# Scores of layers 2 and 3 as sums of one-pass float32r products, with q, k and the row maxima split into halves

## Time and profile before

| | us |
|---|---|
| median of 3 runs | 3493.28 (3492.97 to 3499.72) |
| profiled execution, first to last instruction | 3493.6 |
| of it, from the first to the last maximum of the slots | 1661.1 to 3235.6 |

### The profile page before, as it was taken

One profiled execution on the slowest core, in us unless ns is written; L12 is line 12 of the kernel. 1 busy time (PEld: TensorE's weight loads), 2 busy tenths in 40 slices (PEclk: granted clock), 3 DMA queues, 4 the chain that ended last, 5 costly groups with the idle time before them and its releaser, 6 DMA issues.

```text
span 3493.6 us, 49096 instructions
## 1 busy us (share of the span) xinstructions
PE 3288.6 (94%) x19540; PEld 1805.6 (52%) x19540; DVE 1845.4 (53%) x3843; ACT 1443.6 (41%) x2613; POOL 243.4 (7%) x214
## 2 busy tenths in 40 slices
PE   6899999999889999998999999999999999999887
PEld 3555666656565666666333344444444444453364
DVE  4776544562412232324766765567755666656343
ACT  0344444453412222221355455554555544555433
POOL 1100000100100000001000010010100101001010
PEclk9899999999889999999999999999999999999899
DMA  5200000002000000001000000000000000000000
GB/s 166 90 1 6 8 20 1 23 6 95 16 22 1 0 1 0 1 1 56 1 1 1 1 7 1 4 25 7 7 1 4 22 10 7 1 10 19 7 1 13
DMA packets 57256, 57.99 MB, mean 17 GB/s; under 512 B 17728, under 2 KB 51248, under 8 KB 56764
## 3 DMA queue, kind: packets, MB, share of 16 engines
q1 hardware_dynamic: 57028, 54.79, 5.0%
HBM read 46.89 MB, written 7.89 MB: 16 GB/s over the span
## 4 chain that ended last, share of the span: by engine, by line
PE 88%; DVE 9%; ACT 2%; issue 1%; POOL 0%; DMA 0%; DVEq 0%; SPq 0%; ACTq 0%
PE ps L902 81%; PE ps L1076 3%; DVE max_halves L1565 1%; DVE row_max_cross L1718 1%; PE ps L1203 1%; PE ps L1056 1%; PE ps L1067 1%; DVE big L1590 1%; ACT probs L1944 1%; DVE bn_stats L1619 1%; PE ps L1181 0%; ACT big L1896 0%; DVE bn_stats L1596 0%; DVE xn_tok L1632 0%; DVE big L1724 0%
## 5 line engine op out<-in xcount | busy, mean ns | idle before, releaser
L1896 ACT ACTIVATE big<-ps 128x512 f32<-128x512 f32 x1280 | 687.4, 597 | 826.7 <-PE ps L902 825.9
L902 PE MATMUL ps<-big 32*128 32x512 f32 (+2 forms) x5760 | 940.8, 603 | 16.4 <-DVE row_max L1562 4.3
L1565 DVE TENSOR_REDUCE max_halves<-ps 128x1 f32<-128x512 f32 x1024 | 652.6, 684 | 341.4 <-PE ps L902 340.0
L902 PEld LDWEIGHTS ps<-big 32*128 32x128 f32 (+1 forms) x5760 | 380.8, 188 | 494.5 <-issue 389.6
L902 PE MATMUL ps<-big,probs 128*32 128x512 f32 (+1 forms) x2688 | 379.3, 606 | 8.2 <-ACT big L1896 4.1
L902 PE MATMUL ps<-weights_mlp,big 128*128 128x256 f32 (+1 forms) x1248 | 333.0, 418 | 2.5 <-ACT big L1956 2.5
L902 PEld LDWEIGHTS ps<-weights_mlp,big 128*128 128x128 f32 x1248 | 233.7, 190 | 84.4 <-issue 58.4
L1602 DVE TENSOR_TENSOR x_tok<-ps,x_tok 128x512 f32<-128x512 f32 x112 | 77.2, 690 | 309.0 <-PE ps L902 309.0
L902 PE MATMUL ps<-x_T,weights_mlp 128*128 128x256 f32 x1024 | 231.1, 384 | 2.5 <-ACT x_T L1913 2.3
L1944 ACT ACTIVATE probs<-ps 77x512 f32<-77x512 f32 x384 | 196.1, 591 | 88.3 <-PE ps L902 88.0
L1562 DVE TENSOR_REDUCE row_max<-ps 128x2 f32<-128x512 f32 x256 | 164.6, 684 | 99.7 <-PE ps L902 99.5
(11 more groups left out here) (223 smaller groups left out, 3385.2 us busy)
## 6 DMA issues: line engine op xcount, KB each, us to landing
weights_mlp<-in_L_xcond_mlp_W SPq DMA_DIRECT2D x5, 1024.0 KB, 5.3
weights_mlp<-in_L_xcond_W_mlp SPq DMA_DIRECT2D x5, 1024.0 KB, 5.3
x_tok<-in_x SPq DMA_DIRECT2D x4, 1024.0 KB, 9.4
out_y<-x_tok SPq DMA_DIRECT2D x8, 512.0 KB, 2.9
big<-in_L_xcond_e_w SPq DMA_DIRECT2D x3, 1024.0 KB, 10.1
gates_biases<-mod_rows SPq DMA_DIRECT2D x20, 128.0 KB, 5.0
big<-in_L_xcond_adaLN_W SPq DMA_DIRECT2D x1, 2304.0 KB
kc_groups<-x_tok SPq DMA_DIRECT2D x3, 616.0 KB, 8.4
```

The lines of the kernel that those rows point to most:

```text
L902: return pe.matmul(out, lhsT, rhs, start=first, stop=last)
L1565: dve.tensor_reduce(NMP[:, e, j, qt, hf:hf + 1], PS[:, bank, :], AX.X, ALU.max, negate=True).then_inc(R.frees(key), 1)
L1896: act.activation(PB[:, score % 2, j, :], PS[:, R.bank(key), :], ACT.Exp, scale=SCALE).then_inc(R.frees(key), 1)
```

```diff
-                self.lead = self.per + 2
+                self.split = l == 2
+                self.lead = self.per + (3 if self.split else 2)
...
+            if R.split:
+                return out + [("qk", b, m, a, hf) for m in range(KT) for a, hf in ((1, 0), (1, 1), (0, 0), (0, 1))] + [("v", b, m) for m in range(KT)]
...
+            if kind == "slot" and R.split:
+                return (1.9 if tok[1] is not None else 0.0) + (0.95 if tok[2] is not None else 0.0) + 0.45 * len(tok[4]) + 0.45 * len(tok[5])
             if kind == "slot":
                 return (2.15 if tok[1] is not None else 0.0) + (1.05 if tok[2] is not None else 0.0) + 0.45 * len(tok[4]) + 0.45 * len(tok[5])
...
+                    if tok[0] == "qk" and R.split:
+                        _, b, m, a, hf = tok
+                        n = R.parted.index(tok[1:])
+                        sp.wait_ge(*R.freed(tok))
+                        for x, part in enumerate((0, 1) if a else (0, 1, 0)):
+                            dst = KPd[b, m, :, x, :, hf * HALF:(hf + 1) * HALF] if a else QPd[b, m, hf, :, x]
+                            sp.dma_start(dst, STG[:, n % STAGES, part, :].bitcast(F32)).then_inc(R.part_out[n % STAGES], 16)
+                    if tok[0] == "ld":
+                        n = tok[1]
...
+                        if n >= Q_BLOCKS:
+                            sp.wait_ge(R.pv, (n - Q_BLOCKS + 1) * R.per)
+                        if qh == 0:
+                            for hf in range(NH):
+                                sp.wait_ge(*R.parts_landed(b, m, 1, hf))
...
+                        sp.wait_ge(*R.parts_landed(b, m, 0, qh))
+                        for x in range(2):
+                            sp.dma_start(QR[:, n % Q_BLOCKS, x, :].bitcast(F32), QPd[b, m, qh].rearrange("(j e) x r n -> e j x r n", e=2)[e, :, x:x + 2].rearrange("j x r n -> j (x r) n")).then_inc(R.q_in[n % Q_BLOCKS], 16)
...
+                def by_parts(t, f, half):
...
+                            stationary.append([KR[rows, u, kt * P:(kt + 1) * P]] * 2 + [SUB[rows, :]])
+                            moving.append([QR[rows, n % Q_BLOCKS, 0, :], QR[rows, n % Q_BLOCKS, 1, :], MR[rows, n % 2, :]])
...
+                        stationary.append([QR[rows, n % Q_BLOCKS, x, c:c + P] for x in range(2)])
+                        moving.append([KR[rows, u, hf * HALF:(hf + 1) * HALF]] * 2)
+                    banks = []
+                    for step in range(3):
+                        for i, key in enumerate(keys):
+                            if step == 0:
+                                banks.append(take(key))
+                            if step < len(moving[i]):
+                                last = mm(PS[:, banks[i], :], stationary[i][step], moving[i][step], step == 0, step == len(moving[i]) - 1)
+                                if step == len(moving[i]) - 1:
+                                    done(last, key)
...
+                        elif R.split:
...
+                            dve.wait_ge(R.part_hi, n + 1)
+                            dve.scalar_tensor_tensor(parts[:, 1, :], PS[:, R.bank(tok), 0:w], QB[:, 3 * a, m:m + 1], parts[:, 0, :].bitcast(F32), ALU.add, ALU.subtract).then_inc(R.frees(tok), 1)
...
+                    for n in nms if R.split else ():
+                        if n >= 2:
+                            act.wait_ge(R.pv, (n - 1) * R.per)
+                        act.wait_ge(*R.full(("nm", n)))
+                        copy(MR[:, n % 2, :], PS[:, R.bank(("nm", n)), :]).then_inc(R.frees(("nm", n)), 1)
...
+                            act.wait_ge(*R.full(tok))
+                            if n >= STAGES:
+                                act.wait_ge(*R.parts_landed(*R.parted[n - STAGES]))
+                            act.activation(STG[:, n % STAGES, 0, :], PS[:, R.bank(tok), 0:w], ACT.Identity, bias=QB[:, 3 * a, m:m + 1]).then_inc(R.part_hi, 1)
...
+                    for n in tok[5] if kind == "slot" and R.split else ():
+                        pool.wait_ge(R.nm_f, n + 1)
...
+                        pool.tensor_copy(halves[:, :, ROW_HI:ROW_HI + 4].bitcast(F32R), NMF[:, n % 2]).then_inc(R.nm_h, 1)
+                        pool.wait_ge(R.nm_h, n + 1)
+                        pool.tensor_tensor(halves[:, :, ROW_LO:ROW_LO + 4], NMF[:, n % 2], halves[:, :, ROW_HI:ROW_HI + 4], ALU.subtract).then_inc(R.nm, 1)
```

More of the change, by code:

```diff
@@ L7 @@
 F32 = mybir.dt.float32
+F32R = mybir.dt.float32r
 BF16 = mybir.dt.bfloat16
@@ L459, in slot_token @@
             tails = ((base + t - 2) // R.per,) if 2 <= t < count + 2 and (t - 1) % R.per == 0 else ()
-            nms = ((base + ahead) // R.per - 1,) if 0 < ahead <= count and ahead % R.per == 0 else ()
+            after = ahead - 1 if R.split else ahead
+            nms = ((base + after) // R.per - 1,) if 0 < after <= count and after % R.per == 0 else ()
             return ("slot", base + t if 0 <= t < count else None, base + ahead if ahead < count else None, base + t - 1 if 1 <= t <= count else None, tails, nms)
@@ L551, in open_to @@
                     return rows[tok[-1]] is None
+                if kind == "qk" and R.split:
+                    return True
                 if kind == "qk" and tok[1]:
@@ L577, in slot_ready @@
                 b, g, qh = R.block(fill // R.per)
-                if fill < NB * R.total and fill % R.per == 0 and qh == 0 and g % 2 == 0:
+                if R.split and fill < NB * R.total and fill % R.per == 0:
+                    if ("ld", fill // R.per) not in ended:
+                        return None
+                    times.append(ended["ld", fill // R.per] + 4.0)
+                if not R.split and fill < NB * R.total and fill % R.per == 0 and qh == 0 and g % 2 == 0:
                     for k in R.qk_steps(b, g // 2):
@@ L618, in place, with block_fits @@
                         place(item[0])
+                while R.split and state["ld"] < NB * NG * NH and block_fits(state["ld"]):
+                    state["ld"] += 1
+                    order.append(("ld", state["ld"] - 1))
+                    ended["ld", state["ld"] - 1] = state["now"] + 5.0
+            def block_fits(n):
+                b, g, qh = R.block(n)
+                parts = [("qk", b, g // 2, 0, qh)] + ([("qk", b, g // 2, 1, hf) for hf in range(NH)] if qh == 0 else [])
+                return all(k in ended for k in parts) and (n < Q_BLOCKS or state["t"] > (n - Q_BLOCKS + 1) * R.per)
             def hidden_follows(tok):
@@ L1044, in slot @@
                     for half in range(2):
+                        if R.split:
+                            by_parts(score, fills, half)
+                            if half == 0 and product is not None:
+                                pv(product)
+                            continue
                         if score is not None:
@@ L1066, in slot @@
                             qt = 4 * qh + i
[L1067 removed]
+                            rows = NM[:, q % 2, i:i + P] if R.split else NM[:, 2 * qh + g % 2, qt:qt + P]
+                            last = pe.transpose(PS[:, bank, i * P:(i + 1) * P], rows, ident[:, :])
                         done(last, ("nm", q))
```

81 lines of the change are left out of this document (73 added, 8 removed).

## The result

The changed kernel takes 3471.41 us (median of 6 runs, 3466.34 to 3475.47), the kernel before 3494.59 us beside it (6 runs, 3488.58 to 3500.87): a ratio of 0.9925, 95% interval 0.9906 to 0.9943. It is faster, by 23 us and clear of the interval, where 94 were forecast; the time lies within the stated range (3330 to 3485), the gain is a quarter of the forecast one. The profiled execution has a span of 3464.7 us, 28.9 less than the one before.

The account below looks back on a forecast made before the run. PE was taken to bound the kernel, busy 94% of the span. From 3493.6 us, A -105, B -28, D +29, E +6 and F +5 gave 3400.6, stated as 3400 us, range 3330 to 3485.

Parts of the forecast that it names:

- A: PE's score halves: three rounds of 0.216 us passes, a half 0.86 us in place of 1.07; -105 us.
- Loads inside a half: Weight loads of rounds two and three stay hidden under running passes on PE, costed at nothing.
- the rival built on it: Each round pays 0.10 us for its load, so A and B gain nothing: 3533 us, chance 0.06.
- the slower pass: A float32r pass on PE costs 0.43 us, like a float32 pass: 3695 us, chance 0.07.
- not done: Products run as float32 after all, some 870 us more; left under the slower pass, no chance of its own.
- B: Slots without filler: fourth row gets its bank earlier, slot 3.22 us in place of 3.85; -28 us, bounds 0 and -80.
- F: Maxima split on in-order POOL, so PE's transposes sometimes wait for it: +5 us, 0 to 20.
- E: Later projections: ACT waits for parts to land, holding exponentials and PE: +6 us, 0 to 20.
- 133 waits: PE's waits for exponentials before the change, 110 + 23, 80 us in all; B counted 0.21 us for each.
- that rival: Evacuation by DVE and ACT comes later and eats half of A: 3481 us, chance 0.08.
- D: Start of the region: parts go through DRAM and back before the first maxima and scores: +29 us, 10 to 50.
- 1677 if half of that shows: In D, last landing at 1677 us if half of read-backs' 5.2 us ahead of parts shows, 1683 if all.

Follow-up runs that it names:

- e7: e6 with MLP weights, their biases and the first batch row's cross keys issued behind the second read-back: 3386.67 us, ratio 0.9688.
- e1: Changed kernel with parts laid out in DRAM so part DMAs have 128 or 64 outermost rows, not 8 and 4: 3427.73 us, ratio 0.9815.
- e3: Changed kernel with the two POOL instructions that split the maxima moved to DVE: 3448.51 us, ratio 0.9890.
- e4: Changed kernel with exponentials of layers 2 and 3 on 256 of 512 columns, output not the reference's: 3427.07 us, ratio 0.9808.
- e6: Changed kernel with the edits of e1 and e3, and the first three read-backs later in SP's queue: 3405.51 us, ratio 0.9751.
- e2: Changed kernel without the parts' way through DRAM, fixed rows copied by POOL instead, output not the reference's: 3407.52 us, ratio 0.9762.
- e11: Changed kernel run once more, unedited, one execution: 3474.4 us.
- e10: e6 run once more, unedited, one execution: 3390.2 us.

## Why the prediction was right and wrong

**The direction and the passes (A) were right, the size 13 us off.** A half takes 0.89 us over the trace in place of 0.86: 512 x 0.18 = -92, not -105. The row that failed me is the 0.216 of the earlier trace rows: a float32r pass begins 0.23 to 0.24 after the one before it. I called that row a bf16 product; only its weight loads are bf16, and the columns that it streams stand in the trace before as fp8e4, so it was a farther row than I said:

```profile
80.70 2.17 PE L902 MATMUL ps<-probs,ones_b 128*128 128x512 fp8e4 x8
```

**Loads inside a half were hidden, as I took it.** The first round's loads lie in the open, and the second round begins 0.34 after it; had each round paid like that, the third would begin 0.34 after the second. It begins 0.24 after. The rule that I set against it ("TensorE: Matmul & The Clock Gate" of the Trainium skill, Part 3, The mechanism) doesn't show here, and the rival built on it is out. So are the slower pass and "not done".

**The fourth bank (B) was right in the slot and hardly to be seen in the sum.** The slot without filler took 3.31 where I said 3.22. Summed from each half's first weight load to that of the next thing PE does, halves took 695.7 us before and 604.3 after; less 512 unhindered halves (1.07 and 0.89) that leaves 148 of waiting on either side. In e7, with F gone, E smaller and the clock higher, 116 are left (572.1 - 456): -32. Not all of that is B. Over halves that lie wholly at the higher clock, the waiting is 0.26 us a half before and after, 0.25 in e1, 0.24 in e3 and 0.22 in e7, some 20 us for 512; the rest of the 32 goes with the clock. So some 20 of B's 28 were there, and in the changed kernel the waits that e1 and e3 take away stood in their place. My 133 waits were a little high, too: 7 of the 23 of products are the stops of weight loads, counted twice.

The rows of PE's waits before, over the scored slots (the earlier trace rows shows a shorter stretch):

```profile
PEld ps L902 <- DVE max_halves L1565: 90.0, 121, 4.1
PEld ps L902 <- ACT big L1896: 65.1, 110, 1.6
...
PE ps L902 <- ACT big L1896: 18.7, 27, 1.2
```

With each stop counted once, PE's waits for ACT went from 83 to 91 us, those for DVE's maxima from 92 to 46. So evacuation didn't eat A. The measured time lies in the range that I gave that rival (3455 to 3495, price 3481), but by the start's loss and not by its mechanism. e4 shows what ACT's waits are worth: 44 us, some 9 of them by the clock (24 us less of the low one). That is a bound for a next change.

**The start (D) is the step that failed: +59 for +29, beyond its bound of 50.** The chain as I walked it was right in kind: eight projections, two staging buffers, read-backs ahead of parts in SP's queue. The mis-sized term is the landing. I took 3.0 us from the W_proj load, which is as large but lies across 128 partitions; the parts' DMAs run on 8 and 4 engines and let the waiting engine go 4 to 10 us after their last issue, and four issues took 8.95 us where e1 needs 2.81. So the first maxima, put 21 us later than before, began 49 later (69.1 us into the region in place of 20.0); from there to the first scores the loss was 10, of 8 forecast. With the width mended (e1) landings are near what I had taken, 2.5 to 4.5, the first maxima begin 23 later, and D is 83.3 - 49.4 = +34 against my +29. My upper bound, 50, came from the 616 KB write; it was no bound, since that row told nothing of how a smaller DMA is spread. I had priced a DMA by its size alone. Of the start's 108.8 us, 68 had the lower clock, against 15 of 49.4 before; 44 of them are one stretch from 1674 to 1718 us, in which PE mostly waited. What that cost no run shows.

**The order in SP's queue** I had costed at half, "1677 if half of that shows"; in e1 the fifth part stood ready at 1666.2 and was issued at 1673.6, and e6 got 11 us by moving three read-backs. The weights in front cost 6 more (e7). I had let the first landing take 4.3 from SP's becoming free; I left out that these weights still had to land (ACT had its first landing 2.9 us after the last of four issues in e6, 0.9 in e7).

**Later projections (E): +6 forecast, about +10 found.** e1's slots are 25.7 shorter, with 41 us less of low clock; at 0.39 that is 16, and 10 remain; e2, without the hop, leaves 12 the same way. That DMA is nearly idle there (a share of 0.10), my reason, was true and no help: a read could use only 4 engines.

**Maxima through POOL (F): +5 forecast, about +8 found.** The sign I named (PE's transposes waiting for POOL) stood there, 7 times, 15.1 us. e3's 25.7 less 0.39 x 44 us of low clock is 8. At e11's 0.22 for each us of low clock, E would be 17 and F 16, both still within my bounds; the 15.1 us of waits are F's most direct measure.

**What no step had: the clock.** In the scored slots 17 us more of low clock, some 7 us; ahead of the region 5.4 us that the change doesn't explain, since e1 to e3 begin the region within 0.7 us of the kernel before with the changed kernel's code there (over all runs it begins anywhere from 1640.5 to 1648.4). I had costed every wait by its length and given the clock no term.

The sum again, for the scored slots: A -92, B about -21, four projections moved to the start -7, E +10, F +8, clock +7: -95, of which B is what is left when the others are taken off; the count over halves at the higher clock gives 20 as well. The start +59, ahead of the region +5, after the slots +1. A rests on the trace; E, F and the clock rest on runs and on the 0.39, which one pair of executions gives; the 7 of the projections is the prediction's own figure, not measured.

## What to carry to other kernels

Before you price a DMA by a row of the trace, compare the outermost dimension of its access pattern on both sides, not only its bytes: the same 256 KB took about three times as long to land on 4 or 8 of 16 engines, and a layout in which 128 or 64 rows lie outermost mended it without an instruction more. In a chain through DRAM, look at what stands ahead of each hop in the issuing engine's queue; a read-back that waits for a landing holds every write behind it. And run one program twice before you explain 20 us in a stretch where PE waits now and then: read the granted clock first.

## What the runs showed of the hardware

- A DMA's share of the 16 engines follows its outermost dimension: two tenths and 100 GB/s with 4, five tenths and 200 with 8 (changed kernel, 1668 to 1691 us), up to 9 tenths and 415 GB/s with 64 or 128 (e1, 1660 to 1675 us).
- Successive float32r passes of 512 columns on 32 rows begin 0.23 to 0.24 us apart at the higher clock, where products of 512 fp8e4 columns on bf16 weights began 0.216 apart; their weight loads of 0.18 to 0.19 lie inside the pass before, on the same rows.
- The same program had the lower clock for 27 us of its slots in one execution (e10) and for 82 in another on another chip (e6); the slots were 21 us apart.
